# The first loads in another order, and no constant-tile matmuls behind the first group's transposes

## Chip, cores and metric

The kernel runs on one core of a Trainium2 chip. The metric is the device time in microseconds (us) of one execution; the median over several runs is what is compared.

## What is computed

An attention layer with one head over x of shape (2, 4096, 256), then a residual and a layer norm, then a feed-forward part that replaces the three quarters of the rows with the highest router score, and a second residual and layer norm. Cut to what matters:

```python
def attention(x, w_attn, b_attn, w_proj, b_proj):
    q, k, v = jnp.split(x @ w_attn + b_attn, 3, axis=-1)
    mask = jnp.where(jnp.tril(jnp.ones((T, T), dtype=jnp.bool_)), 0.0, -10000000000.0)
    attn = softmax(jnp.einsum('btc,bsc->bts', q, k) / jnp.sqrt(C) + mask, axis=-1)
    return jnp.einsum('bts,bsc->btc', attn, v) @ w_proj + b_proj

def ffn(x, w_router, w_block):
    scores = jnp.einsum('bld,d->bl', x, w_router)
    _, top_idx = jax.lax.top_k(scores, int(L * 0.75))
    selected = jnp.take_along_axis(x, top_idx[:, :, None], axis=1)
    processed = jax.nn.gelu(jnp.einsum('bkd,de->bke', selected, w_block))
    return x.at[jnp.arange(B)[:, None], top_idx].set(processed)

x = layernorm(x + attention(x, ...))
x = layernorm(x + ffn(x, ...))
```

## The kernel before, in words

The 2 x 4096 rows are cut into 16 groups (G = 0 to 15) of 512 query rows, eight for each batch. Products are made in float32 accuracy out of two rounded parts, a high and a low one: three matmuls stand for one (`split3`, whose matmul is line 587). A = Wq Wk^T and WV = Wv Wproj are formed on the chip at the start, so scores are (x A + u) x^T and values are x WV.

For each group: x^T of the group (two chunks of 128 x 512) is loaded (`project_load`, line 856), ScalarE (ACT) rounds it to the high part (`xhi`, line 876; line 879 for group 0), GpSimd (POOL) makes the low part (line 894), TensorE (PE) makes q (lines 916 and 922 for group 0, then 587), and ACT and VectorE (DVE) bring it to SBUF in two parts (lines 932, 937). Then come the score tiles, one for each 128 keys, each of which ACT copies out of one of two banks into a ring of slots (line 1021). DVE adds the causal mask on diagonal tiles (line 1029) and keeps a running maximum (lines 1056, 1065). `row_max` transposes that maximum on PE (`mt`, line 1111), DVE reduces it (lines 1121 to 1128), and PE spreads it again (`mb`, line 1134). Softmax is z (DVE, 1147), exp (ACT, 1154), high part (ACT, 1161), low part (DVE, 1166), and then PE multiplies with the values (lines 1230 to 1238). After the last group come two layer norms, a search of the router threshold, and the stores.

The operations of each engine are put into named streams (`at(engine, stream, make)`). Each stream keeps its own order. A planner (`merged`, `planned`, lines 256 to 335) runs through them once when the kernel is built, with estimated durations, and writes one fixed order for each engine: among the streams of an engine it takes the operation that can start first, and among those that can start at once the one with the most work behind it, shifted by tables of preferences for each stream. At run time each engine goes through its written order and waits at each operation for its semaphores. SyncE (SP) issues all loads and stores from such an order too, so a wait on SP holds back every transfer written behind it.

At the start (`prepare`) SP issues w_q and w_k, the two chunks of x^T of group 0, the bias columns, then, behind a wait for the first chunk (line 671), w_v, w_proj and b_proj, then w_block and the router's row (broadcast to 128 partitions), then x^T of groups 1 and 2 behind a wait for w_v (line 851), and the first two blocks of x (`attention_out load`, line 1282, the same wait). x^T of groups 1 and 2 goes to slots of the ring, and that of group 3 again to `xraw`.

PE begins with 8 matmuls of a constant bfloat16 tile of ones (`warm`, `busy`, line 647). The same `busy` puts `HELD` = 3 of them behind `mt` and 3 behind `mb` of group 0. Four small jobs hang behind the first four score tiles (`behind_scores`): sums of the keys' and queries' biases (lines 704, 711), the bias row (lines 723, 724), and the column sums of w_block (`block_sums`, line 730). That last one waits for both loads on `ld_ffw` and for DVE's `b_tot` (lines 795, 798). DVE's `block_parts` (804 to 809) and `router_sum` (818) wait for the same loads.

Of the kernel before, what the change touches and what calls it, by code (L numbers as in the profile page):

```python
# [16 lines left out]
P = 128  # L17
B, T, C = 2, 4096, 256
# [21 lines left out]
EARLY = 2  # L40
# [3 lines left out]
WARM = 8  # L44
HELD = 3
STRAIGHT = 3
# [291 lines left out]
def program(nc, x, xt, w_attn_t, columns, w_proj, b_proj, w_router, w_block, out):  # L338
# [46 lines left out]
    for f in out_fills:  # L385
        kind, G, j = f
# [4 lines left out]
    for f in late_fills:  # L391
        kind, G, j = f
# [11 lines left out]
    with ctx:  # L404
        sb = lambda name, shape, dt=F32: ctx.enter_context(nc.sbuf_tensor(name, shape, dt))
        psum = lambda name: ctx.enter_context(nc.psum_tensor(name, [P, 512], F32))
        sem = lambda name: ctx.enter_context(nc.semaphore(name))
# [88 lines left out]

        ld_qk, ld_b, ld_w, ld_ffw, ld_xt = sem("ld_qk"), sem("ld_b"), sem("ld_w"), sem("ld_ffw"), sem("ld_xt")
        ld_xt0 = [sem(f"ld_xt0_{n}") for n in range(EARLY + 1)]
        ld_xh, a_xh0, ld_wv = [sem("ld_xh0"), sem("ld_xh1")], sem("a_xh0"), sem("ld_wv")
# [155 lines left out]
        def prepare():  # L655
# [12 lines left out]
            def load_w(sp):  # L668


                sp.wait_ge(ld_xh[0], 16)
                sp.dma_start(wv_t, wt_rows[2]).then_inc(ld_wv, 16)
                sp.dma_start(wp, w_proj.rearrange("(k p) c -> p k c", p=P)).then_inc(ld_w, 16)
                sp.dma_start(bp_row, b_proj.rearrange("(a c) -> a c", a=1)).then_inc(ld_w, 16)

            def load_block(sp):
                sp.dma_start(wb, w_block.rearrange("(k p) c -> p k c", p=P)).then_inc(ld_ffw, 16)
                sp.dma_start(wr[:, :], w_router.rearrange("(a c) -> a c", a=1).broadcast_to([P, C])).then_inc(ld_ffw, 16)
            at("sp", "prepare", load_qk)
# [3 lines left out]
            at("sp", "prepare", load_w)  # L683
            at("sp", "prepare", load_block)

# [39 lines left out]
            def block_sums(pe):  # L725
                pe.wait_ge(ld_ffw, 32)
                pe.wait_ge(g_const, 2)
                pe.wait_ge(v_btot, 1)
                for k in range(CC):
                    mm = pe.matmul(w_sums, ones[:, :], wb[:, k, :], start=k == 0, stop=k == CC - 1)  # L730
                mm.then_inc(p_wsum, 1)
# [9 lines left out]
            pe_fill["values weights"] = [lambda pe, m=m, k=k: values_weights(pe, m, k) for m in range(CC) for k in range(CC)]  # L741
            behind_scores.extend([[lambda pe: query_sums(pe, 0)], [lambda pe: query_sums(pe, 1), bias_product], [bias], [block_sums]])

# [56 lines left out]
            def block_parts(dve):  # L800
                dve.wait_ge(ld_ffw, 32)
                dve.wait_ge(p_wsum, 1)

                dve.scalar_tensor_tensor(out=wb, in0=w_sums[:, None, :].broadcast_to([P, CC, C]), scalar=-1.0 / C, in1=wb,
                                         op0=ALU.mult, op1=ALU.add).then_inc(v_wb, 1)
                dve.wait_ge(v_wb, 1)
                dve.tensor_copy(WB[:, 0], wb).then_inc(v_wb, 1)
                dve.wait_ge(v_wb, 2)
                dve.tensor_tensor(WB[:, 1], wb, f32(WB[:, 0]), ALU.subtract).then_inc(v_wb, 1)
# [6 lines left out]
            def router_sum(dve):  # L816
                dve.wait_ge(ld_ffw, 32)
                dve.tensor_reduce(sum_w[:, :], wr[:, :], AX.X, ALU.add).then_inc(v_sw, 1)
# [8 lines left out]
            def bias_load(sp):  # L827
                sp.wait_ge(st_b, 16)
                sp.wait_ge(v_wdiff, 1)
                for k in range(CC):  # L830
                    sp.dma_start(b_cols[:, k:k + 1], b_dram[k * P:(k + 1) * P].rearrange("(p a) -> p a", a=1)).then_inc(ld_bc, 16)
            at("sp", "bias columns", bias_store)
            at("sp", "bias columns", bias_load)
# [12 lines left out]
        def project_load(G):  # L846
            b, g = groups[G]

            def load(sp):
                if G <= EARLY:  # L850
                    sp.wait_ge(ld_wv, 16)
                if G == EARLY + 1:
                    xlo_made(sp, 0)
                elif G > EARLY:
                    xlo_made(sp, G - 1)
                sp.dma_start(raw_of(G), xt_rows[b][:, :, g * GQ:(g + 1) * GQ]).then_inc(ld_xt0[G] if G <= EARLY else ld_xt, 16)
            at("sp", "project load", load)

# [402 lines left out]
        def attention_out(G):  # L1261
# [7 lines left out]
            def load(sp):  # L1269
                if G == len(groups) - 1:  # L1270

                    sp.wait_ge(p_s, n_tiles)
                    filled(sp, ("v", G, 1))
                elif G >= 2:
                    sp.wait_ge(st_x1[G % 2], 16 * (G // 2))
                    sp.wait_ge(v_hw, QT * (G - 1))
                    sp.wait_ge(g_y, 2 * (G - 1))
                    if not upright(G - 2):
                        filled(sp, ("ft", G - 2, 1))
                else:  # L1280
                    sp.wait_ge(ld_wv, 16)
                sp.dma_start(r, x_rows[b][:, tile0:tile0 + QT, :]).then_inc(ld_x[G % 2], 16)
# [763 lines left out]
        for G in range(len(groups)):  # L2046
            ordered[:] = [G]
            if G:
                project_load(G)
# [127 lines left out]
```

## Time and profile before

| | |
|---|---|
| median of 3 runs | 954.7 us (954.55 to 959.75) |
| the profiled execution, first to last instruction | 953.7 us |
| TensorE busy | 931.6 us, 98% of it |
| VectorE busy | 785.4 us, 82% |
| ScalarE busy | 633.7 us, 66% |
| GpSimd busy | 305.0 us, 32% |
| DMA | 155.84 MB, mean 163 GB/s |

The profile is of one execution. Its span runs from the first to the last instruction, and the median of the runs is 1.0 us above it. A busy share is an average over the whole span, so what an edit of the first 40 us is worth is to be read in the rows of those 40 us, and then from what the rest of the kernel does with work that comes earlier.

### The profile page before, as it was taken

What the parts mean: (1) busy time and instruction counts of PE and PEld (TensorE: products, weight loads), DVE (VectorE), ACT (ScalarE), POOL (GpSimd) and SP (SyncE); (2) the same over time, 40 slices, a digit from 0 to 9 for tenths busy, and PEclk for the clock granted to TensorE, in tenths of its full rate; (3) what the DMA queues carried; (4) which work ended last, traced back from release to release, by engine and by line L of the source; (5) the groups of instructions that cost most, each with busy time, mean ns of one, the idle gap of its engine ahead of it and who ended that gap; (6) DMA issues with size and microseconds to landing.
All of it is one profiled execution on the core that took longest, in us unless ns stands there. A gap on an engine that the chain in (4) does not pass through costs nothing.

```text
span 953.7 us, 15684 instructions
## 1 busy us (share of the span) xinstructions
PE 931.6 (98%) x5030; PEld 798.6 (84%) x5030; DVE 785.4 (82%) x1497; ACT 633.7 (66%) x1011; POOL 305.0 (32%) x460
## 2 busy tenths in 40 slices
PE   9999999999999999999999999999999999999992
PEld 6889998888888888888888999888888888888871
DVE  5898887866994896589879999998699799659977
ACT  3576665864774594479565866677578569547994
POOL 3541141242230335333325361452022244301243
PEclk9999999999999999999999999999999999999996
DMA  6644344344353355468634534346777734437934
GB/s 193 206 123 154 104 144 122 103 144 152 101 185 113 111 155 175 146 205 263 195 104 149 189 93 142 130 123 207 234 238 226 242 113 134 150 105 238 323 124 177
DMA packets 89044, 155.84 MB, mean 163 GB/s; under 512 B 8442, under 2 KB 18300, under 8 KB 88964
## 3 DMA queue, kind: packets, MB, share of 16 engines
q1 hardware_dynamic: 88964, 154.85, 51.0%
q8 instruction: 41, 0.67, 0.3%
q14 instruction: 39, 0.32, 0.1%
HBM read 114.96 MB, written 39.86 MB: 162 GB/s over the span
## 4 chain that ended last, share of the span: by engine, by line
PE 85%; DVE 7%; ACT 4%; issue 2%; DMA 1%; DVEq 0%; SPq 0%; ACTq 0%
PE sbank L587 37%; PE fbank L587 12%; PE obank L1236 9%; PE obank L1237 9%; PE obank L1238 9%; PE obank L1232 2%; PE obank L1230 2%; PE obank L1231 2%; DVE ring L1147 1%; ACT parts L1161 1%; DVE ring_lo L1166 1%; ACT ring L1154 1%; DMA ring<-xt 1%; DVE tail L2037 1%; PE mbank L1134 1%
## 5 line engine op out<-in xcount | busy, mean ns | idle before, releaser
L587 PE MATMUL sbank<-qT,xT 128*128 128x512 f32 (+2 forms) x1728 | 406.6, 377 | 1.1 <-ACT ring L1021 1.0
L587 PEld LDWEIGHTS sbank<-qT,xT 128*128 128x128 f32 x1728 | 306.4, 188 | 54.9 <-ACT ring L1021 1.1
L1021 ACT COPY ring<-sbank 128x512 f32<-128x512 f32 (+3 forms) x286 | 157.2, 553 | 178.3 <-PE sbank L587 125.1
L1166 DVE TENSOR_TENSOR ring_lo<-ring,parts 128x1024 fp32r<-128x1024 f32 (+4 forms) x174 | 181.1, 1050 | 32.2 <-ACT parts L1161 31.4
L1161 ACT CAST parts<-ring 128x1024 fp32r<-128x1024 f32 (+4 forms) x174 | 145.0, 843 | 48.1 <-PE obank L1238 34.1
L1070 DVE TENSOR_TENSOR runmax<-ring,runmax 128x1024 f32<-128x1024 f32 x84 | 107.1, 1274 | 69.0 <-ACT ring L1021 68.1
L1147 DVE TENSOR_TENSOR ring<-ring,mbank 128x1024 f32<-128x1024 f32 (+4 forms) x174 | 157.0, 955 | 5.6 <-PE mbank L1134 5.3
L1236 PE MATMUL obank<-ring_lo,vs 128*128 128x512 f32 (+3 forms) x416 | 158.9, 382 | 0.2 <-DVE ring_lo L1166 0.2
L1238 PE MATMUL obank<-parts,vs 128*128 128x512 f32 (+3 forms) x416 | 157.4, 378 | 0.0
L1237 PE MATMUL obank<-parts,vs 128*128 128x512 f32 (+3 forms) x416 | 157.4, 378 | 0.0
L1154 ACT ACTIVATE ring<-ring 128x1024 f32<-128x1024 f32 (+4 forms) x174 | 142.2, 852 | 9.7 <-DVE ring L1147 9.5
L1238 PEld LDWEIGHTS obank<-parts,vs 128*128 128x128 f32 x416 | 78.2, 188 | 14.6
L1236 PEld LDWEIGHTS obank<-ring_lo,vs 128*128 128x128 f32 x416 | 78.3, 188 | 14.3 <-issue 0.9
L1237 PEld LDWEIGHTS obank<-parts,vs 128*128 128x128 f32 x416 | 78.3, 188 | 13.3
L1674 POOL TENSOR_TENSOR yb<-xres,yb 128x512 f32<-128x512 f32 x28 | 39.1, 1418 | 140.2 <-ACT yb L1595 76.5
L1291 POOL TENSOR_TENSOR xres<-xres,b_tot 128x512 f32<-128x512 f32 x30 | 44.5, 1505 | 55.5 <-DMA xres<-x 53.1
L894 POOL TENSOR_TENSOR xT<-xraw,xT 128x512 fp32r<-128x512 f32 x27 | 37.9, 1422 | 64.4 <-ACT xT L876 63.4
L1570 POOL TENSOR_TENSOR ot_sb<-ot_sb,yb 128x512 f32<-128x512 f32 x16 | 22.6, 1413 | 102.5 <-PE fbank L1328 80.1
L587 PE MATMUL fbank<-WV,xT 128*128 128x256 f32 x384 | 51.5, 284 | 0.0
L1065 DVE TENSOR_TENSOR runmax<-ring,runmax 128x512 f32<-128x512 f32 (+3 forms) x73 | 43.3, 594 | 9.7 <-ACT ring L1021 7.6
L587 PEld LDWEIGHTS fbank<-WV,xT 128*128 128x128 f32 x384 | 49.6, 191 | 1.7
L587 PE MATMUL fbank<-xT,A 128*128 128x512 f32 x180 | 46.1, 392 | 0.2 <-DVE qT L937 0.2
(268 smaller groups left out, 1371.4 us busy)
## 6 DMA issues: line engine op xcount, KB each, us to landing
vs<-v_scratch SPq DMA_DIRECT2D x288, 256.0 KB, 2.9
v_scratch<-vnew SPq DMA_DIRECT2D x30, 512.0 KB, 3.5
out<-tail SPq DMA_DIRECT2D x32, 256.0 KB, 2.6
xres<-x SPq DMA_DIRECT2D x15, 512.0 KB, 3.9
x_scratch<-xres SPq DMA_DIRECT2D x14, 512.0 KB, 3.9
y_scratch<-yb SPq DMA_DIRECT2D x14, 512.0 KB, 3.0
tail<-x_scratch SPq DMA_DIRECT2D x28, 256.0 KB, 3.6
tail<-y_scratch SPq DMA_DIRECT2D x28, 256.0 KB, 4.3
```

The lines of the kernel that those rows point to most:

```text
L587: mm = eng.matmul(o, lhs(lh, k), rhs(rh, k), start=n == 0, stop=n == len(todo) - 1)
L1021: act.copy(slot(n)[:, c0:], sbank[n % NSS][:, c0:]).then_inc(a_copy, 1)
L1065: dve.tensor_tensor(runmax[:, 0, c0:], slot(n)[:, c0:], runmax[:, 0, c0:], ALU.max).then_inc(v_max, 1)
L1070: dve.tensor_tensor(runmax[:, :, :], slots(ns, 0), runmax[:, :, :], ALU.max).then_inc(v_max, 1)
L1147: dve.tensor_tensor(slots(ns, c0), slots(ns, c0), mbank[:, None, c0:].broadcast_to([P, len(ns), GQ - c0]), ALU.subtract).then_inc(v_z, 1)
L1154: act.activation(slots(ns, c0), slots(ns, c0), ACT.Exp, scale=SCALE).then_inc(a_exp, 1)
L1161: act.copy(hi_of(u), slots(ns, c0)).then_inc(a_hi, 1)
L1166: dve.tensor_tensor(slots_lo(ns, c0), slots(ns, c0), f32(hi_of(u)), ALU.subtract).then_inc(v_lo, 1)
L1236: pe.matmul(o, vh, lo_, start=n == first_tile[G], stop=False)
L1237: pe.matmul(o, vh, hi_, start=False, stop=False)
L1238: mm = pe.matmul(o, vl, hi_, start=False, stop=last)
L1291: pool.tensor_tensor(r[:, 2 * j:2 * j + 2], r[:, 2 * j:2 * j + 2], b_tot[:, None, :].broadcast_to([P, 2, C]), ALU.add).then_inc(g_xres, 1)
```

## The change

Three edits in one.

1. The order of the first loads. The wait for the first chunk of x^T ahead of w_v goes. x^T of groups 1 and 2 is issued right behind b_proj, in SP's `prepare` stream, with no wait. w_block gets a stream of its own and waits until x^T of group 1 has landed. The router's row gets one too, with a semaphore of its own (`ld_wr`), and waits until x^T of group 2 has landed, as do the first two loads of x.
2. `HELD` goes from 3 to 0: no constant-tile matmuls behind `mt` and `mb` of group 0.
3. `block_sums` leaves the list behind the score tiles for a PE stream of its own, "prepare block". It and `block_parts` wait for w_block alone, and `router_sum` for the router's row alone.

The order of every engine is planned anew from this.

```diff
-HELD = 3
+HELD = 0
@@
+        ld_wr = sem("ld_wr")
@@
             def load_w(sp):
-
-
-                sp.wait_ge(ld_xh[0], 16)
                 sp.dma_start(wv_t, wt_rows[2]).then_inc(ld_wv, 16)
                 sp.dma_start(wp, w_proj.rearrange("(k p) c -> p k c", p=P)).then_inc(ld_w, 16)
                 sp.dma_start(bp_row, b_proj.rearrange("(a c) -> a c", a=1)).then_inc(ld_w, 16)

             def load_block(sp):
+                sp.wait_ge(ld_xt0[1], 16)
                 sp.dma_start(wb, w_block.rearrange("(k p) c -> p k c", p=P)).then_inc(ld_ffw, 16)
-                sp.dma_start(wr[:, :], w_router.rearrange("(a c) -> a c", a=1).broadcast_to([P, C])).then_inc(ld_ffw, 16)
+
+            def load_router(sp):
+                sp.wait_ge(ld_xt0[2], 16)
+                sp.dma_start(wr[:, :], w_router.rearrange("(a c) -> a c", a=1).broadcast_to([P, C])).then_inc(ld_wr, 16)
@@
             at("sp", "prepare", load_w)
-            at("sp", "prepare", load_block)
@@
             def block_sums(pe):
-                pe.wait_ge(ld_ffw, 32)
+                pe.wait_ge(ld_ffw, 16)
@@
-            behind_scores.extend([[lambda pe: query_sums(pe, 0)], [lambda pe: query_sums(pe, 1), bias_product], [bias], [block_sums]])
+            behind_scores.extend([[lambda pe: query_sums(pe, 0)], [lambda pe: query_sums(pe, 1), bias_product], [bias]])
+            at("pe", "prepare block", block_sums)
@@
             def block_parts(dve):
-                dve.wait_ge(ld_ffw, 32)
+                dve.wait_ge(ld_ffw, 16)
@@
             def router_sum(dve):
-                dve.wait_ge(ld_ffw, 32)
+                dve.wait_ge(ld_wr, 16)
@@
+            for n in range(1, EARLY + 1):
+                project_load(n)
+            at("sp", "prepare block", load_block)
+            at("sp", "prepare router", load_router)
@@
             def load(sp):
-                if G <= EARLY:
-                    sp.wait_ge(ld_wv, 16)
@@
-            at("sp", "project load", load)
+            at("sp", "prepare" if G <= EARLY else "project load", load)
@@ attention_out load
-                    sp.wait_ge(ld_wv, 16)
+                    sp.wait_ge(ld_xt0[2], 16)
@@
-            if G:
+            if G > EARLY:
                 project_load(G)
```

## Rows read from the trace of the kernel before

**Rows 1.** The page: busy time and share of the span, by engine.
```profile
PE 931.6 (98%) x5030; PEld 798.6 (84%) x5030; DVE 785.4 (82%) x1497; ACT 633.7 (66%) x1011; POOL 305.0 (32%) x460
```
**Rows 2.** Windows: stretch, its us, busy us of each engine, granted PE clock, DMA share, GB/s.
```profile
12.60:17.50 4.90, 3.92 (x24) 3.60 (x24) 1.96 (x4) 1.51 (x3) 0.39 (x1) 1.00 1.05 371
17.50:23.00 5.50, 5.26 (x34) 4.34 (x35) 5.11 (x14) 2.47 (x7) 2.53 (x3) 1.00 0.29 101
30.00:900.00 870.00, 869.13 (x4678) 750.70 (x4677) 727.80 (x1307) 582.38 (x911) 272.89 (x374) 1.00 0.51 162
900.00:930.00 30.00, 28.66 (x172) 22.84 (x171) 23.71 (x94) 29.97 (x64) 11.79 (x28) 1.00 0.49 174
930.00:954.00 24.00, 6.08 (x38) 3.20 (x36) 18.55 (x57) 10.18 (x23) 7.27 (x18) 0.66 0.47 175
```
**Rows 3.** The chain that ended last, first 32 us: start us, us, what.
```profile
8.60 7.36 DMA ring<-xt
...
23.20 0.65 PE obank L647 x3
23.85 5.61 PE fbank L587 x36
...
29.89 0.65 PE obank L647 x3
30.54 0.86 PE obank L730 x4
```
**Rows 4.** Timeline of ACT: start us, us, instruction [idle before, releaser].
```profile
10.41 1.27 ACT L932 ACTIVATE qT<-fbank,ucol 128x512 fp32r<-128x512 f32 x2 [3.23 <-PE fbank L922]
15.98 1.04 ACT L876 CAST xT<-ring 128x1024 fp32r<-128x1024 f32 x1 [4.31 <-DMA ring<-xt]
16.94 0.96 ACT L1021 COPY ring<-sbank 128x512 f32<-128x512 f32 x2
```
**Rows 5.** Timeline of PE, 1 to 23 us.
```profile
1.04 3.59 PE L647 MATMUL obank<-ones_bf 128*128 128x512 bf16 x8 [1.04 <-POOL ones_bf L2106]
...
12.64 1.62 PE L587 MATMUL sbank<-qT,xT 128*128 128x512 f32 x6
...
17.57 0.98 PE L587 MATMUL sbank<-qT,xT 128*128 128x256 f32 x6 [1.00 <-ACT ring L1021]
...
22.55 0.66 PE L1111 MATMUL mbank<-ident,runmax 128*128 128x128 f32 x4 [0.17 <-DVE runmax L1065]
```
**Rows 6.** Timeline of DVE, 11 to 30 us.
```profile
11.13 1.41 DVE L937 SCALAR_TENSOR_TENSOR qT<-fbank,ucol,qT 128x512 fp32r<-128x512 f32 x2 [1.97 <-ACT qT L932]
...
22.86 0.15 DVE L798 TENSOR_SCALAR b_tot<-b_tot 128x1 f32<-128x1 f32 x1
...
29.09 0.74 DVE L937 SCALAR_TENSOR_TENSOR qT<-fbank,ucol,qT 128x512 fp32r<-128x512 f32 x1
```
**Rows 7.** Timeline of SP: issues of transfers.
```profile
2.76 0.43 SPq L663 DMA_DIRECT2D bcols<-columns  x1
5.90 0.38 SPq L672 DMA_DIRECT2D ring<-w_attn_t  x1
...
7.24 0.38 SPq L677 DMA_DIRECT2D ring<-w_block  x1
```
**Rows 8.** DMA issues of the first 20 us: count, KB each, median us to landing.
```profile
xraw<-xt SPq DMA_DIRECT2D x2, 256.0 KB, 4.2
...
wr<-w_router SPq DMA_DIRECT2D x1, 128.0 KB, 6.9
```
**Rows 9.** Windows of the first loads (columns as in rows 2).
```profile
2.00:6.00 4.00, 4.00 (x11) 2.03 (x10) 0.00 (x0) 0.16 (x2) 2.98 (x21) 1.00 0.83 258
...
12.00:16.00 4.00, 3.91 (x24) 3.28 (x22) 2.51 (x5) 0.01 (x1) 0.00 (x0) 1.00 0.99 360
```
**Rows 10.** Groups by form, whole run: count, busy us, mean ns, idle before.
```profile
L1166 DVE TENSOR_TENSOR ring_lo<-ring,parts 128x1024 fp32r<-128x1024 f32 x112 | 145.1, 1302 | 28.5 <-ACT parts L1161 28.1
...
L1161 ACT CAST parts<-ring 128x1024 fp32r<-128x1024 f32 x112 | 116.9, 1053 | 31.6 <-PE obank L1238 28.2 <-PE obank L1232 3.2
```

## Prediction

> **What bounds the kernel now.** I read the page's busy times first. TensorE is busy for 931.6 of 953.7 us [rows 1], so at most 22.1 us of the span are not its own work. The windows then say where these lie: from 30 to 900 us PE is busy for all but 0.87 of 870 us, and only behind 900 do 1.34 and 17.92 us open, in the tail [rows 2]. So from 30 to 900 us the kernel is one dense stream of matmuls. What lets PE reach 30 us earlier should reach the end undiminished, and what eases another engine there gives nothing. All the rest of this change lies ahead of 31 us, and two stretches of it have holes: 12.6 to 17.5 (3.92 of 4.90) and 17.5 to 23 (5.26 of 5.50) [rows 2].
>
> The chain of work that ended last shows what makes them. It does not go over PE there: it goes from the first chunk of x^T to w_v, issued at 5.90 [rows 7], whose landing lets x^T of group 1 be issued at 8.60, and that takes 7.36 us, to 15.96 [rows 3]. The timeline of ACT tells who suffers: ACT's written order has the rounding of group 1 (line 876) ahead of the copy of score tile 0 (line 1021). It stands still for 4.31 us, rounds from 15.98 to 17.02, and only then copies the tile [rows 4]. That tile was finished on PE at 12.64 + 1.62 = 14.26 us [rows 5]. As there are two score banks, PE waits 1.00 us for the copy before tile 2, and 0.17 us more before `mt`, at the end of DVE's running maximum, which began late for the same reason [rows 5].
>
> **The change, part by part.**
>
> *Loads.* w_v is no longer held until 5.90: its issue follows the bias columns, at 2.76 + 0.43 = 3.19 us. From w_v to where w_block was issued took 7.24 - 5.90 = 1.34 us for three issues [rows 7], so x^T of group 1 is issued at about 4.5 us instead of 8.60, and group 2 at about 5.0. When does it land? Low bound by the rate: 2 x 256 KB of weights, 2 x 256 KB of x^T, 2 x 256 KB of w_v and w_proj, and its own 512 KB are 2.1 MB. At the 360 GB/s of 12 to 16 us, from 2 us on, this is 5.8 us, so 7.8; at the 258 GB/s of 2 to 6 us it is 10.1 [rows 9]. High bound: its own former 7.36 us from issue to landing [rows 3], 11.9. The former time contained w_block and the router's row ahead of it. The row alone took 6.9 us for 128 KB [rows 8], and both now stand behind. I take 9 to 10. All of these are ahead of 14.26, and with 1.04 us of rounding even 11.9 gives 12.9. So ACT is free when tile 0 is ready, and PE's 1.00 us goes. Group 2, 512 KB later, lands 1.5 to 2 us after (0.52 MB by either rate) and costs ACT 1.06 us in a stretch where it has stood for 4.31.
>
> Then `mt`. PE runs about 1.0 us earlier from tile 2. DVE's running maximum has some 2.7 us more, since tile 0's copy (0.96 / 2 us [rows 4]) can end at 14.74 and not at 17.42 (16.94 + 0.48).  I take the 0.17 us as gone too: PE's own work sets `mt`. Sum of this part: 1.00 + 0.17 = 1.17 us. Bounds: nothing, if another wait stands in its place, and 1.22 us, all of the two holes (0.98 + 0.24) [rows 2].
>
> What does the removed wait protect? It kept w_v and w_proj off the wires until the first chunk of x^T was in. The two chunks take a median of 4.2 us from issue to landing [rows 8]; the first is rounded at once. If 512 KB shared the rate with them evenly, they could be 0.52 MB / 258 GB/s = 2.0 us later. The row of 258 GB/s at a DMA share of 0.83 [rows 9] leaves room, and w_v's issue at 3.19 is behind both chunks. I take 0, and keep 2.0 less some 1.2 us of time that PE spends on A's products and key sums meanwhile, 0.8 us, for the range. The Trainium skill, DMA: Bandwidth & Descriptors, section Queues, rings and completion order, says that each DMA engine consumes the descriptors of one issuing queue in ring order. By that rule the later weights cost the chunks nothing, and the sum stays 2.5 us; by even sharing it would be 1.7. No row here tells the two apart.
>
> *Constant matmuls.* Each three cost 0.65 us on the chain, at 23.20 and at 29.89, with PE work right behind both [rows 3]. Nothing hides them: the matmuls behind the first belong to values and q whose inputs are there (36 of line 587 in one piece of 5.61 us), and behind the second comes `block_sums`. The second has a condition. Score tile 4 needs the low part of q of group 1, ended at 29.09 + 0.74 = 29.83 [rows 6], and `mb` ends at 29.89. Both are driven by PE's work ahead of them, so both move by the same 1.8 us, and the tile finds its q ready by 0.06 us only if `block_sums` (0.86 us) is no longer between. So I count 2 x 0.65 = 1.30 us, with 0.65 as the low bound (the second lost to a wait for q) and 1.30 as the high one.
>
> *`block_sums`.* The same four matmuls, 0.86 us [rows 3], somewhere else on PE: 0 in the sum. If the plan puts it ahead of `mt`, PE waits for `b_tot`, which DVE ended at 22.86 + 0.15 = 23.01 [rows 6], against `mt` at 22.55: up to 0.5 us, for the range. Its other input, w_block, issued when group 1's x^T is in (12 at the latest) with 6.9 us as the worst row for a smaller load [rows 8], is there by 19.
>
> *SP.* Behind the new waits stand w_block, the router's row, the first two loads of x and x^T of group 3. `block_sums` read w_block at 30.54, and POOL takes x only behind `mb`, at 29.89 [rows 3]: all of it is hidden by the 17 us that are left even from 13 us on. Without that cover a late x would hold up only the residual, far from PE.
>
> The sum: 1.17 + 1.30 = 2.47 us. The profiled span 953.7 would be 951.2. The median stands 1.0 above the span, so 954.7 becomes 952.2.
>
> **Rivals.**
>
> *A, the new order costs a softmax pass (slower).* All engines are planned anew, and I cannot read the new order from this trace. Place: the last two groups, where the tail behind 900, with holes of 1.34 and 17.92 us on PE, hangs on ACT and DVE [rows 2]. If one step of the last groups is written one unit too late, PE or the tail waits for a pass over 1,024 columns: the low part 1.302 us and the high part 1.053 [rows 10], z and exp taken at the same two values: 4.7 us. 952.2 + 4.7 = 956.9. It decides once the new waits exceed 2.5 us. For it: the tail has no cover. Against: a shift that is the same for all engines leaves most of a plan as it was. Chance 0.20.
>
> *B, ACT takes the roundings ahead of q.* If x^T of group 1 and 2 are written ahead of line 932, then q of group 0, which ACT started at 10.41 [rows 4], waits for the landing: with 11.9 and 1.04 of rounding until 12.9, 2.5 us on the way to tile 0, for which DVE's 12.54 [rows 6] is just in time. Result 954.7. With a landing at 9.4 or earlier it costs nothing. Against it: before, the roundings stood behind q. Chance 0.05.
>
> *C, nothing arrives.* The holes go elsewhere (tile 4's q, a bank), 0.65 to 2.5 us are spent again, 954.7. Chance 0.15.
>
> *D, the clock.* The granted clock reads 1.00 in all windows up to 930 [rows 2], and the first 8 constant matmuls nevertheless take 3.59 / 8 = 0.45 us each against 0.65 / 3 = 0.22 later [rows 3, 5], so such a fall is 1.2 for 2.4 GHz. If it fell behind `mb` for as long as that opening, 3.59 us, half of it is lost: 1.8 us, 954.0. Against it: through the hole of 1.00 us the clock stayed at 1.00, and the change leaves PE with less idle time. The Trainium skill, TensorE: Matmul & The Clock Gate, section HAM oscillation, warns that waits between bursts of matmuls make the clock fall, which would speak for the fillers; the trace has no wait there for them to fill. Chance 0.03.
>
> **How the numbers follow.** The forecast (1.5 to 3.5 us gained) holds 0.54, A 0.20, C 0.15, B 0.05, D 0.03, and 0.03 are left for an order that also closes later holes. Low end: PE's holes from 30 to 930, 0.87 + 1.34 = 2.2 us [rows 2], closed as well: 950.0, taken to 949.5. High end: A with the 0.5 us of `block_sums`, 957.4, taken to 957.5. One per cent, about what a measurement of this kernel can tell from no change, is 9.5 us. Only a tail written anew reaches that far: faster 0.02, slower 0.05, within 0.93.
>
> **What would show each step.** Right: x^T of group 1 lands by 12 us; ACT copies tile 0 at 14.3 to 14.8; no wait before tile 2; `mt` at 21.3; line 647 has 8 matmuls; score tile 4 begins about 2.5 us earlier than 30.54 + 0.86 = 31.40 (give or take `block_sums`); PE from there to 900 as dense as before. Wrong: ACT's line 932 later than 10.4; a PE wait before `mt` or tile 4; PE's holes from 30 to 930 above 2.2 us, or a tail longer than before, with the early gain intact.

## The result, and the profile after

| | before | after |
|---|---|---|
| median, 17 runs of each | 954.83 us (953.89 to 959.75) | 959.4 us (958.45 to 960.26) |
| ratio of the times | 1 | 1.0044, 95% interval 1.0035 to 1.0053 |
| the profiled execution | 953.7 us | 956.7 us |

The change makes the kernel 0.44% slower. It had been forecast 0.3% faster. Both are within one per cent, but 959.4 lies outside the range (949.5 to 957.5) and on the other side.

The page's busy times of after hardly differ from [rows 1]: the work is the same. VectorE has grown by 6.2 us and GpSimd by 2.4, the others have shrunk by less than one.

```profile
PE 931.4 (97%) x5024; PEld 798.3 (83%) x5024; DVE 791.6 (83%) x1497; ACT 633.0 (66%) x1011; POOL 307.4 (32%) x460
```

The windows say where PE stands still. The first two and the last three answer to [rows 2], with the same columns; the three in the middle are cut around a hole (stretch, its us, busy us of PE, PE's weight loads, DVE, ACT, POOL, granted clock, DMA share, GB/s).

```profile
12.60:17.50 4.90, 4.54 (x30) 4.31 (x31) 3.60 (x9) 2.28 (x4) 0.82 (x1) 1.00 0.90 269
17.50:23.00 5.50, 5.50 (x36) 4.64 (x35) 2.71 (x12) 1.60 (x4) 0.00 (x0) 1.00 0.10 35
...
42.00:44.00 2.00, 0.26 (x2) 0.00 (x0) 2.00 (x3) 0.69 (x1) 2.00 (x2) 1.00 0.00 0
44.00:46.00 2.00, 1.90 (x8) 1.65 (x9) 1.90 (x4) 0.18 (x1) 0.47 (x1) 0.88 0.26 41
46.00:49.00 3.00, 3.00 (x16) 3.00 (x16) 2.90 (x6) 1.00 (x2) 0.00 (x0) 0.51 0.42 153
...
30.00:900.00 870.00, 865.53 (x4654) 747.28 (x4654) 731.61 (x1304) 577.78 (x905) 277.59 (x374) 1.00 0.51 160
900.00:930.00 30.00, 28.94 (x170) 23.24 (x168) 24.43 (x89) 29.97 (x60) 11.59 (x32) 1.00 0.59 206
930.00:957.00 27.00, 8.83 (x53) 5.34 (x52) 20.82 (x65) 13.21 (x30) 8.47 (x19) 0.75 0.42 156
```

The two early stretches are as forecast: PE's idle time in them falls from 0.98 + 0.24 us to 0.36 + 0. But from 30 to 900 us, where before had 0.87 us of holes, after has 4.47. The sums of the waits name what is new, 1.84 and 1.75 us (who waits for whom: us in total, times, longest; the first sum also holds the 0.44 us before tile 0):

```profile
PE sbank L588 <- issue: 2.3, 2, 1.8
PE mbank L1138 <- DVE mcol L1132: 1.9, 2, 1.8
```

And the timeline of PE places them. Rows of the first 30 us stand beside those of [rows 5].

```profile
12.96 1.62 PE L588 MATMUL sbank<-qT,xT 128*128 128x512 f32 x6 [0.44 <-issue]
...
16.74 0.96 PE L588 MATMUL sbank<-qT,xT 128*128 128x256 f32 x6
...
19.12 3.14 PE L588 MATMUL fbank<-WV,xT 128*128 128x256 f32 x24
22.10 2.91 PE L588 MATMUL fbank<-xT,A 128*128 128x512 f32 x12
24.84 1.60 PE L588 MATMUL fbank<-WV,xT 128*128 128x256 f32 x12
26.28 2.21 PE L588 MATMUL sbank<-qT,xT 128*128 128x128 f32 x12
28.32 0.60 PE L1115 MATMUL mbank<-ident,runmax 128*128 128x128 f32 x4
...
44.10 1.68 PE L588 MATMUL sbank<-qT,xT 128*128 128x512 f32 x6 [1.84 <-issue]
45.58 2.76 PE L588 MATMUL fbank<-WV,xT 128*128 128x256 f32 x12
...
74.96 0.65 PE L1138 MATMUL mbank<-ident,mcol 128*128 128x128 f32 x4 [1.75 <-DVE mcol L1132]
```

Three things are to be seen. Tile 2 (16.74) has no wait before it, as forecast. `mt` of group 0, forecast at 21.3, stands at 28.32 and not at 22.55: between them PE has done group 1's q and three units of values' projection, and only then the last score tile of group 0 (in the piece at 26.28). And the two large holes, 1.84 and 1.75 us, lie at 42.3 and 73.2 us, the time of groups 1 and 2, far from the start and from the tail. Behind the first of them 12 projection matmuls take 2.76 us instead of the 1.60 that they took at 24.84: the granted clock is 0.51 from 46 to 49 us, 1.2 GHz in place of 2.4.

The starts of `mt` and `mb` of each group make a ruler for the whole kernel (timelines of PE, us):

| | before | after | both edits, old order |
|---|---|---|---|
| `mt`, group 0 | 22.55 | 28.32 | 21.42 |
| `mt`, group 1 | 47.31 | 48.14 | 44.79 |
| `mb`, group 1 | 49.85 | 50.73 | 47.33 |
| `mb`, group 2 | 77.85 | 74.96 | 75.33 |
| `mt`, group 3 | 111.49 | 114.51 | 108.98 |
| `mt`, group 5 | 241.96 | 245.04 | 239.45 |
| `mt`, last group | 862.37 | 865.41 | 860.50 |

From group 3 on, after is later by a constant 3.0 us. Whatever is lost is lost before 112 us. (Group 2's softmax comes earlier in after because its place among the matmuls is another.) The third column is an experiment, told next.

### The profile page after: what moved, and what is told of

Read it like the earlier page. It is cut to its first block, busy times and chain, and to the rows that moved or that the text cites. A ratio compares the mean times of both kernels' runs of the same rounds, so it can differ in the third digit from the quotient of the medians.

```text
span 956.7 us, 15672 instructions
## 1 busy us (share of the span) xinstructions
PE 931.4 (97%) x5024; PEld 798.3 (83%) x5024; DVE 791.6 (83%) x1497; ACT 633.0 (66%) x1011; POOL 307.4 (32%) x460
## 4 chain that ended last, share of the span: by engine, by line
PE 86%; DVE 7%; ACT 4%; issue 2%; DMA 0%; SPq 0%; DVEq 0%; ACTq 0%
PE sbank L588 37%; PE fbank L588 13%; PE obank L1240 9%; PE obank L1241 9%; PE obank L1242 9%; PE obank L1236 2%; PE obank L1234 2%; PE obank L1235 2%; DVE ring L1151 1%; ACT parts L1165 1%; DVE ring_lo L1170 1%; ACT ring L1158 1%; DVE tail L2041 1%; PE mbank L1138 1%; PE mbank L1115 1%
## 5 line engine op out<-in xcount | busy, mean ns | idle before, releaser
L1074 DVE TENSOR_TENSOR runmax<-ring,runmax 128x1024 f32<-128x1024 f32 x84 | 109.4, 1302 | 64.4 <-ACT ring L1025 63.6
L1240 PEld LDWEIGHTS obank<-ring_lo,vs 128*128 128x128 f32 x416 | 78.3, 188 | 14.3 <-issue 0.9
```

The source lines that it names most:

```text
L1074: dve.tensor_tensor(runmax[:, :, :], slots(ns, 0), runmax[:, :, :], ALU.max).then_inc(v_max, 1)
L1240: pe.matmul(o, vh, lo_, start=n == first_tile[G], stop=False)
```

## Experiments

Two theories stood against each other, and a third beside them. **The order**: the edits of the loads and fillers gain what was forecast, and the planner's new order loses more (theories marked O, where a letter is used). **The edits**: the loads collide with something or the fillers were needed, whatever the order. **The clock** (C): a good part of the loss is the stretch at half clock behind the hole.

What parts them is a kernel with its order *pinned*: the list of streams that the planner wrote for one version is stored, and another version is built by it. All pinned kernels have this edit (the stored list is cut here); it fixes the order in which the program is written and nothing else.

```diff
-    orders, times = planned(todo, signalled, urgency(todo), favours)
+    orders, times = pinned(), {}    # the stored order of another version
...
```

### The edits, with the order of before

**p_loads**: the new order of first loads alone. PE, DVE, ACT and POOL keep before's order; SP has the moved loads.

> The new order of loads alone (HELD stays 3, block_sums stays behind score tile 3), with every engine's written order fixed to that of the kernel before (on SP only the moved loads stand elsewhere). Theory O (the loss is in the planned order, the edits themselves save time): PE's waits of 1.00 and 0.17 us before score tile 2 and mt go, nothing else moves, so 1.2 us faster: ratio 0.9988. Theory D (the loads themselves hurt, since w_v and w_proj now share the wires with the first x^T and the bias columns): PE waits 0.4 us or more before line 697 or later, and the time is the same or up to 1 us longer.

**p_both**: the new loads, `HELD = 0`, and `block_sums` in its old place, in before's order.

```diff
-HELD = 3
+HELD = 0
```

> The new order of loads and HELD = 0, block_sums behind score tile 3, every engine's order fixed to that of the kernel before. Theory O: 1.2 + 1.3 = 2.5 us faster than before, ratio 0.9974, the sum of the prediction. Theory C (the constant-tile matmuls kept the clock up): the granted clock falls below 1.00 somewhere between 20 and 60 us, and at least half of the 2.5 us is lost again.

**p_held**: `HELD = 0` alone, in before's order, with the old loads.

> HELD = 0 alone, loads and orders as before. Theory O: 1.3 us faster, ratio 0.9986, and the wait before score tile 2 (1.00 us) stays. Theory C: clock below 1.00 behind mt or mb, gain under 0.7 us.

**p_held3A**: the reverse. After's order is pinned, and the constant matmuls are put back.

```diff
-HELD = 0
+HELD = 3
```

> The changed kernel with HELD = 3 again, every engine's order fixed to that of the changed kernel. Theory O: the order costs what it costs with or without the fillers: the holes of 1.84 us (before score tile 12) and 1.75 us (before the third mb) stay, the clock falls behind the first of them as without fillers, and the time is 0.7 to 1.3 us above the changed kernel's: 5 to 6 us above before, ratio 1.0055. Theory C: with the fillers the clock stays at 1.00 from 20 to 80 us, and the time falls to within 2.5 us of before.

The four ran on one chip, beside 29 runs of before (median 954.69 us):

| | us, median (range) | ratio, 95% interval |
|---|---|---|
| p_loads | 954.28 (953.83 to 955.21) | 0.9994 (0.9983 to 1.0005) |
| p_both | 953.2 (952.55 to 953.67) | 0.998 (0.9969 to 0.999) |
| p_held | 953.59 (951.92 to 954.57) | 0.9981 (0.9969 to 0.9994) |
| p_held3A | 960.94 (959.76 to 961.23) | 1.0057 (1.0038 to 1.0075) |

With the old order the edits gain: 1.5 us by p_both, 1.1 by p_held. The loads alone, in p_loads, give 0.4 us, which can't be told from nothing (0.9983 to 1.0005), where 1.2 had been expected, though in its profile too both waits are gone (tile 2 at 16.48 and `mt` at 21.05, neither with a wait). In p_both PE has tile 2 and `mt` without a wait, `mt` at the forecast's 21.3:

```profile
16.85 0.95 PE L628 MATMUL sbank<-qT,xT 128*128 128x256 f32 x6
...
21.42 0.60 PE L1154 MATMUL mbank<-ident,runmax 128*128 128x128 f32 x4
```

and its window from 30 to 900 us is as dense as before's, 1.12 us of holes against 0.87 in [rows 2]:

```profile
30.00:900.00 870.00, 868.88 (x4676) 750.15 (x4675) 726.71 (x1306) 582.95 (x911) 272.21 (x373) 1.00 0.52 162
```

Its ruler stands 2.5 us ahead of before from `mb` of group 1 to `mt` of group 5, and 1.9 at the last group. That this is the 2.47 us of the sum is in part luck: tile 0 starts 0.42 us later here (13.06 against 12.64). In the median 1.5 us arrive. In p_held both waits of before stay, 0.18 and 0.17 us here, and `mb` of group 1 is 1.77 us earlier:

```profile
17.13 0.98 PE L627 MATMUL sbank<-qT,xT 128*128 128x256 f32 x6 [0.18 <-ACT ring L1061]
...
22.11 0.66 PE L1151 MATMUL mbank<-ident,runmax 128*128 128x128 f32 x4 [0.17 <-DVE runmax L1105]
```

(The wait before tile 2 hangs on a landing that moves from run to run. In the four traces with the old loads x^T of group 1 is rounded from 15.98, 15.55, 14.70 and 16.37 us, and the wait is 1.00 in before, 0.18 here, nothing in held_only and 1.33 in block_only.) p_held3A is slower than after itself by 1.5 us (960.94 against 959.4), about the 1.30 that the fillers take, so putting them back cures nothing. Its sum of waits before `mb` has the same long one as after's:

```profile
PE mbank L1178 <- DVE mcol L1172: 2.8, 3, 1.8
```

So the first two edits are worth -1.5 us and the new order some +6 (959.4 against 953.2, on two chips whose medians of before are 0.1 us apart). The third edit, the new place of `block_sums`, is in that order and not in p_both. The theory that the loads or the missing fillers cost the time falls.

### Where the new order loses

**p_fill**: after's order, with 8 constant matmuls put into the hole at 42 us, so that PE is busy while it waits. It separates the hole from the clock that falls behind it.

```diff
+                if (G, m) == (2, 1):
+                    pe_fill[("q", G, m)].append(lambda pe: busy(pe, obank[1][:, :], 8))
```

> The changed kernel with its orders fixed, and 8 constant-tile matmuls (about 1.7 us) put into the hole of 1.84 us that PE has before score tile 12, behind the second half of q of the third group. The hole stays as time, only filled. Theory C (the fall of the clock behind that hole, seen in the changed kernel's profile as 0.50 for some 3 us, is part of the loss): the clock stays at 1.00, and the time is 1.0 to 1.6 us under the changed kernel's 959.4. Theory O2 (the fall is rare or is made up by a later wait, since the 17 runs of the changed kernel at mean clocks of 0.990 to 0.993 do not differ in time): 959.4 within 0.5.

**p_lock**: after's order, with one operation of ACT moved, the rounding of x^T that releases POOL's subtraction. POOL then no longer runs over the small operations of `row_max` of group 2.

```diff
 ('softmax hi', 5)
-('project xhi', 7)
 ('scores copy', 24)
 ('scores copy', 25)
+('project xhi', 7)
 ('softmax hi', 6)
```

> The changed kernel with its orders fixed, but on ACT the rounding of x^T of the seventh group moved behind the next two score copies, so that POOL's two subtractions (1.25 us each) begin behind DVE's two small operations before the third mb. Theory L (those two took 1.09 and 1.19 us instead of 0.16 because POOL held the shared port, and PE waited 1.75 us for them): they take 0.16 us, the wait before the third mb goes, and the time is 1.5 to 1.8 us under 959.4. Rival: the two operations wait for something else, or PE's time is lost again before the next group: 959.4 within 0.5.

**p_fill_lock**: both.

> Both of the two edits above. Theory C + L: 2.5 to 3.4 us under 959.4, leaving only the hole of 1.84 us itself: about 956.5, ratio to before 1.002. Theory O2 + L: 957.8. If neither holds: 959.4.

**after_nudge**: after, planned anew with one more entry in the planner's table of preferences. It makes the first projection of group 0's values ready 0.5 us later in the plan, and nothing else; the chip does not wait for it.

```diff
+        favours["pe", "proj", 8] = (0, 0.5)
```

> The changed kernel, planned anew as it is, with one difference: the planner may not start the first values projection of group 0 until 0.5 us after its inputs. That turns one choice at 17.4 us of the plan (score tile 3 before that projection, as in the kernel before). Theory O (this one choice starts the loss): mt at about 21.4 us instead of 28.3, no PE hole over 0.5 us before 900 us, 2.0 to 2.5 us faster than before less what its remaining new order costs: 952.5 to 954, ratio 0.998. Rival (any new order costs some 4 us, whichever it is): 956 or more.

These ran beside 24 runs of before (median 954.68 us):

| | us, median (range) | ratio, 95% interval |
|---|---|---|
| p_fill | 959.26 (958.1 to 960.46) | 1.0043 (1.0028 to 1.0059) |
| p_lock | 958.03 (957.28 to 958.75) | 1.0031 (1.002 to 1.0041) |
| p_fill_lock | 958.24 (957.6 to 959.07) | 1.0034 (1.0023 to 1.0045) |
| after_nudge | 953.95 (953.38 to 954.72) | 0.999 (0.9981 to 0.9999) |

p_fill is no faster than after (1.0043 against 1.0044), though the clock now stays at 1.00. With six runs over 2.4 us its interval alone would still allow for a gain of 1 us; the traces below decide. First its timeline of PE, then its window:

```profile
43.18 1.90 PE L688 MATMUL obank<-ones_bf 128*128 128x512 bf16 x8
45.18 1.62 PE L628 MATMUL sbank<-qT,xT 128*128 128x512 f32 x6
...
51.71 0.65 PE L1180 MATMUL mbank<-ident,mcol 128*128 128x128 f32 x4 [0.88 <-DVE mcol L1174]
```

```profile
46.00:49.00 3.00, 2.85 (x21) 2.51 (x20) 2.86 (x6) 1.17 (x2) 0.00 (x0) 1.00 0.65 179
```

With PE at full speed it reaches `mb` of group 1 too early and waits 0.88 us there for DVE. At half clock DVE had that time, and no such wait shows in after. The slow stretch of 3 us loses 1.5 us of PE's work, and what it loses is waited for otherwise: from tile 0 to `mb` of group 1 PE takes 37.77 us in after and 37.77 in p_qfirst (told below), where the clock falls, and 37.67, 37.69 and 37.85 in p_fill, p_fill_lock and p_lock, where it does not. The clock as a separate cause falls: what costs is that the order gives PE nothing that is ready.

p_lock closes the hole before `mb` of group 2. Here are the rows of DVE and POOL in after, around both holes:

```profile
41.65 2.82 POOL L898 TENSOR_TENSOR xT<-xraw,xT 128x512 fp32r<-128x512 f32 x2 [3.11 <-ACT xT L880]
41.73 1.61 DVE L1069 TENSOR_TENSOR runmax<-ring,runmax 128x384 f32<-128x384 f32 x1
...
43.26 0.74 DVE L941 SCALAR_TENSOR_TENSOR qT<-fbank,ucol,qT 128x512 fp32r<-128x512 f32 x1
...
72.39 2.50 POOL L898 TENSOR_TENSOR xT<-xraw,xT 128x512 fp32r<-128x512 f32 x2 [12.36 <-ACT xT L880]
72.59 1.09 DVE L1130 TENSOR_TENSOR mcol<-mcol,row_const 128x4 f32<-128x4 f32 x1
...
73.72 1.19 DVE L1132 TENSOR_TENSOR mcol<-mcol,row_const 128x4 f32<-128x4 f32 x1
```

and the second place in p_lock:

```profile
73.30 0.16 DVE L1170 TENSOR_TENSOR mcol<-mcol,row_const 128x4 f32<-128x4 f32 x1
73.50 0.16 DVE L1172 TENSOR_TENSOR mcol<-mcol,row_const 128x4 f32<-128x4 f32 x1
...
73.75 0.61 PE L1178 MATMUL mbank<-ident,mcol 128*128 128x128 f32 x4
...
75.46 2.55 POOL L938 TENSOR_TENSOR xT<-xraw,xT 128x512 fp32r<-128x512 f32 x2 [14.70 <-ACT xT L920]
```

Two operations on 4 columns take 1.09 and 1.19 us while POOL's two subtractions run, and 0.16 us each when they run later. Each is about as long as one of POOL's (2.50 / 2 = 1.25). The Trainium skill, SBUF — State Buffer, section SBUF: two separate sides, says that a DVE operation with two inputs in SBUF and a GpSimd operation that reads SBUF exclude each other for a whole instruction. The trace agrees: 2.28 us instead of 0.32, and PE waits 1.75 of the difference. Without it the kernel is 1.4 us faster than after by the medians (958.03 against 959.4; two chips, and the intervals of the ratios overlap); on one chip p_fill_lock is 1.0 us under p_fill (958.24 against 959.26), and from tile 0 to `mt` of group 3 PE takes 100.32 us in p_lock against 101.55 in after. So it is worth 1.0 to 1.4 us, somewhat under the 1.5 to 1.8 expected. The same overlap stands at 41.7 us: 384 columns of running maximum take 1.61 us beside POOL, while the two operations of 512 columns at 45.84 take 1.42 together. q of group 2 (line 941) stands behind them, and score tile 12 behind q. What share of the hole is its doing no run shows.

after_nudge has all three edits of the change, and a plan in which score tile 3 is again ahead of the values' projection. Everything behind that choice is planned anew too. `mt` of group 0 stands at 21.86, and the holes from 30 to 900 us are 0.80 us:

```profile
21.86 0.60 PE L1115 MATMUL mbank<-ident,runmax 128*128 128x128 f32 x4
```

```profile
30.00:900.00 870.00, 869.20 (x4678) 750.75 (x4677) 728.68 (x1308) 583.57 (x911) 272.14 (x373) 1.00 0.52 162
```

One number in the planner, and the change turns from 4.6 us slower to 0.7 faster. So the loss hangs on the order that was written, and not on what the edits do.

### Each edit alone, planned anew

**loads_only** has the new loads with `HELD = 3` and `block_sums` behind tile 3. **held_only** has `HELD = 0`. **block_only** has the third edit:

```diff
-            behind_scores.extend([[lambda pe: query_sums(pe, 0)], [lambda pe: query_sums(pe, 1), bias_product], [bias], [block_sums]])
+            behind_scores.extend([[lambda pe: query_sums(pe, 0)], [lambda pe: query_sums(pe, 1), bias_product], [bias]])
+            at("pe", "prepare block", block_sums)
```

> The new order of loads alone, planned anew (HELD 3, block_sums behind score tile 3). In its plan score tile 3 of PE stands behind the projections, as in the changed kernel, but values of tile 0 stand before the second half of q of group 2, so the plan has no hole there. Theory O (holes, not the order as such, cost): no PE wait of over 0.5 us before score tile 12, and 954 to 955.5, by the planner's own clock 0.2 us above before. Theory M (mt of group 0 at 28 instead of 22 us costs whatever stands behind it): 957 or more.

> HELD = 0 alone, planned anew, loads as before. Its plan keeps tile 3 ahead of the projections, but has a hole of 1.79 us before mt of group 1, which the plan of before has not. Theory O: the 1.3 us saved are given back there, and the time is 954.5 to 956.5; by the planner's own clock, which adds a slow clock behind such a hole, 957.9. With the order fixed the same edit gave 953.6. Rival (the new plan is as good as the fixed one): 953.6.

> block_sums in a stream of its own alone, planned anew. Both theories: as before, 954.7 within 0.5; it moves from behind mb of group 0 to between score tiles 5 and 6, with no hole. If it were what costs, 956 or more.

**p_qfirst** is after's order with ACT's q of group 0 ahead of the rounding of group 1, rival B undone:

```diff
 ('project xhi', 1)
-('project xhi', 2)
 ('project qhi', 0)
 ('project qhi', 1)
+('project xhi', 2)
 ('project xhi', 3)
```

> The changed kernel with its orders fixed, but on ACT the rounding of x^T of group 1 stands behind q of group 0, as in the kernel before. Theory B (q waited for that rounding, 0.44 us of PE's time in the changed kernel's profile and 1.0 to 1.3 in those of two experiments with the same order): 0.3 to 1.0 us under 959.4. If PE's time is lost again at the hole before score tile 12: 959.4 within 0.3.

They ran beside 33 runs of before (median 954.98 us). The planner gives an end of its own for each version, and the table sets its change beside the measured one:

| | us, median (range) | ratio, 95% interval | change: plan | measured |
|---|---|---|---|---|
| loads_only | 956.6 (956.26 to 957.4) | 1.0012 (1.0003 to 1.0021) | +0.2 | +1.6 |
| held_only | 958.13 (957.26 to 960.78) | 1.0029 (1.0017 to 1.0042) | +3.2 | +3.2 |
| block_only | 955.8 (954.45 to 958.94) | 1.0008 (0.9996 to 1.0021) | 0.0 | +0.8 |
| p_qfirst | 958.55 (958.25 to 959.8) | 1.0034 (1.0023 to 1.0045) | | +3.6 |
| after | 959.4 | 1.0044 | +3.9 | +4.6 |
| after_nudge | 953.95 | 0.999 | -1.3 | -0.7 |

Each edit, planned by itself, is slower or the same, although `HELD = 0` gains with the order held and the loads lose nothing. `HELD = 0` alone is the clearest: -1.1 us in the old order, +3.2 in its own. Its long wait is at another place than after's, 64.05 to 65.83 us (sums of the waits of held_only):

```profile
PE fbank L587 <- DVE row_const L980: 2.2, 2, 1.8
```

Its plan had the hole, 1.79 us, before `mt` of group 1, where the chip has 0.26. That plan and measurement both say +3.2 is so in part luck. loads_only lies between its two expectations, and held_only above that of theory O. There is no single bad edit, and the three plans have different holes.

loads_only shows rival B, q behind the rounding on ACT, at 1.08 us:

```profile
13.98 0.47 PE L588 MATMUL sbank<-qT,xT 128*128 128x512 f32 x1 [1.08 <-ACT qT L935]
```

p_qfirst takes that away from after. Tile 0 then starts with no wait,

```profile
12.74 1.61 PE L628 MATMUL sbank<-qT,xT 128*128 128x512 f32 x6
```

and the kernel gains 0.85 us by the medians (958.55 against 959.4). This is not clear of the noise: two different chips, and the intervals of the ratios overlap (1.0023 to 1.0045, 1.0035 to 1.0053). In the two profiles tile 0 starts 0.22 us apart, and from there to `mt` of group 3 both take the same time (101.58 and 101.55 us). block_only can't be told from no change. Its profiled execution has a hole of 1.3 us at a copy and a fallen clock behind it; in it only, so this says nothing of its median.

```profile
20.00:30.00 10.00, 10.00 (x48) 8.55 (x48) 4.69 (x17) 2.59 (x5) 5.11 (x5) 0.70 0.17 59
```

## Why the prediction was wrong, point by point

**Why the order changed.** This is read from the plan itself, built once for before and once for after. About 17.4 us into the plan PE becomes free and has two candidates: score tile 3, and the first projection of group 0's values, which wants a column sum from DVE. The planner adds 0.6 us of margin to such an input. Before: 17.16 + 0.6 = 17.76, PE free at 17.32, so tile 3 goes first. After: x^T of group 1 lands earlier, POOL's subtraction moves out of the way of DVE's first mask, the sum ends 0.52 us earlier, 16.64 + 0.6 = 17.24, and PE is free at 17.42. Now both can start at once, the one with more work behind it wins, and that is the projection (483 against 475). The next four units win the same way:

```
before: tile 3, v(0,0), mt, v(0,1), q(1,0), q(1,1), v(1,0), mb, ...
after:  v(0,0), v(0,1), q(1,0), q(1,1), v(1,0), tile 3, tile 4, mt, ...
```

`mt` comes 6 us later, and the values of group 0 begin at 58.75 us on PE instead of 43.42. They were the work that PE did while q of group 2 was being made. At 42.3 us there is nothing in their place. The plan of after has that hole too, 2.8 us at 40.4.

The late `mt` alone does not do this. loads_only takes the same choice, its `mt` stands still later, at 30.21, and its values begin at 43.15, with no hole before tile 12. What differs is `block_sums`. The first values of group 0 wait for `v_wb` (line 1226), which DVE's `block_parts` gives, and that waits for `block_sums`. In its own stream, the third edit, `block_sums` is written late on PE, and `block_parts` later still on DVE, so that at 42.3 us the values may not start. First after, then loads_only, where it hangs behind tile 3 as before:

```profile
39.85 1.02 PE L731 MATMUL obank<-ring,ones 128*128 128x256 f32 x4
47.17 0.68 DVE L806 SCALAR_TENSOR_TENSOR ring<-obank,ring 128x512 f32<-128x512 f32 x1
58.75 0.28 PE L1234 MATMUL obank<-vs,ring_lo 128*128 128x256 f32 x1
```

```profile
27.90 1.08 PE L731 MATMUL obank<-ring,ones 128*128 128x256 f32 x4
29.67 0.68 DVE L805 SCALAR_TENSOR_TENSOR ring<-obank,ring 128x512 f32<-128x512 f32 x1
43.15 0.28 PE L1233 MATMUL obank<-vs,ring_lo 128*128 128x256 f32 x1
```

In after_nudge, which has the third edit, `block_sums` stands at 28.35 and the values begin at 41.38. In block_only it stands at 35.90, the values begin at 46.48, and no hole follows. So the loss needs both: after_nudge shows that it hangs on the order that grows from the choice at 17.4 us, loads_only that this choice with an early `block_sums` costs 1.6 us and not 4.6, and the rows of after that the late `block_sums` holds the values back. No run moves `block_sums` or that wait and keeps the rest of after, so what it is worth by itself is not shown. The plan alone makes it much: planned without the wait for `v_wb`, the kernel after has no hole at 40.4, though tile 3 stays behind the projections, and its planned end is 1.3 us before that of before.

**The steps that were right.**
- *Loads.* x^T of group 1, forecast to land at 9 to 10, is rounded from 9.79 us, where [rows 4] has 15.98. Tile 0 is copied at 14.62 (forecast 14.3 to 14.8). The wait before tile 2 is gone, and so is the one before `mt`. The rows of ACT in after:

```profile
9.79 1.05 ACT L880 CAST xT<-ring 128x1024 fp32r<-128x1024 f32 x1 [2.46 <-DMA ring<-xt]
10.74 1.26 ACT L936 ACTIVATE qT<-fbank,ucol 128x512 fp32r<-128x512 f32 x2
...
14.62 0.58 ACT L1025 COPY ring<-sbank 128x512 f32<-128x512 f32 x1 [1.69 <-PE sbank L588]
```

- *The fillers.* p_held gives 1.1 us for their 1.30.
- *The removed wait protected little.* The two first chunks of x^T land 4.1 us behind their issue in after, 4.2 in p_loads and p_both, 4.6 in loads_only and 4.7 in after_nudge (medians of the two), against 4.2 in [rows 8]. The term was put at 0, with 0.8 us for the range.
- *What reaches 30 us earlier reaches the end*, or later: the 3.0 us of after are constant from group 3 to the last.
- *Rival D.* The clock did not need the fillers: it is at 1.00 in p_held up to the tail. It does fall in after, but behind a hole that the order made.

**The steps that failed.** The first is this sentence: "A shift that is the same for all engines leaves most of a plan as it was." The shift was not the same for all: what moved in the plan was one landing, with it POOL's subtraction, and behind that one sum on DVE, by 0.5 us, and a choice between two candidates is a threshold. On that sentence hung the chance of 0.20 for rival A, though its time of 956.9 was the nearest to the truth. Its kind was right, an order that makes PE wait for other engines. Its place was wrong: it was sought in the tail behind 900 us, and PE's idle time from 900 to 930 is even less than before (1.06 us against 1.34). The loss lies between 40 and 76 us. Its size was too small: 4.7 us above the forecast, and 6.2 was measured (959.4 against 953.2). By the profiles of after and p_both, 4.9 us apart in span and at the last group's `mt`, it is 1.84 + 1.75 us of holes and 1.5 at half clock, 5.1 in all. (The 0.44 us before tile 0 are no part of it: this execution was so much earlier that tile 0 starts at 12.96, in p_both at 13.06.)

The second is the term for `block_sums`: "somewhere else on PE: 0 in the sum". The prediction asked what `block_sums` waits for, and not who waits for it. It went from 30.38 to 39.85 us, and the values of group 0, which wait for it through `block_parts`, could not fill the hole at 42.3.

**Terms that were mis-sized.**
- *Loads* (1.17 us). p_loads measured 0.4, and with the fillers' 1.1 the two edits give 1.5 for 2.47. The 1.17 us were the waits of one execution, 0.7 us slower than the typical one (953.7 against 952.95, below); 1.17 - 0.75 = 0.4 would account for it, but that this is the whole reason is an estimate. The waits before tile 2 of 0 to 1.33 us with the same loads speak for it.
- *Rival B* (chance 0.05, "with a landing at 9.4 or earlier it costs nothing"). ACT did take a rounding ahead of q. With the rounding at 9.79 q began at 10.74, and PE waited 0.44 us before tile 0; in loads_only, rounding at 10.80, 1.08, and in after_nudge 0.59. Undoing it gave 0.85 in the medians, not clear of the noise.
- *The third hole*, `mb` of group 2, was no step of the prediction at all. It is a collision of POOL with two operations of 0.16 us, and is worth 1.0 to 1.4 us.
- *The high end.* It was worked out from one softmax pass. An order can lose at several places, and here it lost at three.
- *The median against the span.* The prediction added 1.0 us. In all results here an execution's time is about 1.75 us above its span (958.45 against 956.7), so that the profiled 953.7 of before was itself 0.7 us above its typical span. With 1.75 and 952.95 the forecast would have been 952.2 just the same; what it cost is in the term for the loads above.

**What stays open.** By the medians, the holes that were removed one by one account for 1.4 (p_lock) and 0.85 us (p_qfirst, within the noise) of 6.2. No kernel removes the hole at 42 us or the 0.88 us before `mb` of group 1 and keeps the rest of after's order; after_nudge removes them by another order. In the profile of p_lock PE waits 1.61 us at the first, 0.57 before `mt` of group 1 and 0.91 before `mb`. Of the 6.2 us, 1.4 + 0.85 + 1.61 + 0.57 + 0.91 = 5.3 have a place, and some 0.9 us have none. Nor does any kernel take the third edit away from after or add it to p_both.

The version that beats both is p_both: the first two edits, built by the order of the kernel before, 0.2% faster than before (0.998, 0.9969 to 0.999).

## What to carry to other kernels

Where a planner or scheduler writes the order, the price of an edit is that of the edit plus that of the new order, and the second can be the larger: measure the edit with the old order pinned, then let the order be rewritten and look for new holes. Look first for what an earlier input will overtake, a choice between two operations that can both start, and ask which later wait the overtaken one was to cover. Of an operation that is moved, ask not only what it waits for but who waits for it, through every engine. Take a wait from several traces, where a landing sets it. And a tiny VectorE operation between two TensorE steps can cost a whole GpSimd instruction when one happens to run (1.09 and 1.19 us for 0.16 here).

## What the runs showed of the hardware

- **Clock.** A hole of 1.84 us at 42.3 us was followed by half clock from 46 to 49 us in the profile of after, and the same hole in p_qfirst by a fall too (0.62 from 46 to 49 us). The hole of 1.61 us at that place in p_lock and in p_held3A was not, nor that of 1.75 us at 73.2 us in after or of 1.78 at 64 us in held_only. But behind the hole of 1.33 us in block_only, at 16.6 us, it fell, to 0.50 from 20 to 26 us, so the length alone does not decide, and what does is open. The ruler in block_only stands 3.1 us behind before's at `mt` of group 3, and three of its 12 executions (958.0 to 958.94 us) have a mean clock of 0.988 to 0.990, the others 0.992 to 0.993. Three of the 29 of before that ran beside p_both look alike (957.85 to 959.19 us, 0.987 to 0.989), and none of the 12 of p_both does. That the wait before tile 2 is behind those too is likely, but no trace shows it.
- **The first landings move from run to run.** With the same loads the rounding of x^T of group 1 began at 9.79 us in after, at 10.86 in p_fill and at 11.98 in p_both (there ACT does q first). With the new loads and a good order the times scatter less: 952.55 to 953.67 for p_both, against 953.78 to 959.19 for before on the same chip.
- **The router's row lands late for its size.** Broadcast to 128 partitions, 128 KB, it took 6.9 us to land before and 5.6 after, where 256 KB of w_block took 3.4 and 2.7. Other loads were under way beside it, so that the broadcast is the reason is not shown.
